# Zero rows up to 128 partitions for the scores and replications of a Mamba, attention and MoE kernel

## The reference

```python
# 1: Mamba over the 1024 pixels of an image, group norm, residual
xh = silu(causal_conv_k2(x @ W_in[:, :128]));  z = x @ W_in[:, 128:]
dt = softplus((xh @ W_x[:, :4]) @ W_dt + b_dt)          # 128 channels
h  = exp(dt * A) * h + dt * B * xh                       # 16 states per channel
y  = (sum_n h * C + xh * D) * silu(z);  x = x + silu(group_norm(y @ W_out))
# 2: causal attention over 1024 tokens, 8 heads of 8
t = t + softmax(mask(q @ k.T / sqrt(8))) @ v @ w_proj    # of layer_norm(t)
# 3: mixture of 8 experts, the best 2 of each token
t = t + sum_top2(p * (x @ expert_w + expert_b))          # of layer_norm(t)
```

## Time and profile before

| What | Value |
|---|---|
| median of three runs | 1631.68 us |
| the profiled execution: its own time | 1626.1 us |
| its span in the trace | 1624.0 us |
| TensorE matmul (PE) busy | 1260.7 us, 78% |
| VectorE (DVE) busy | 1171.9 us, 72% |
| ScalarE (ACT) busy | 704.3 us, 43% |
| GpSimd (POOL) busy | 512.2 us, 32% |
| mean granted TensorE clock | 0.761 of 2.4 GHz |
| DMA queues of the kernel | 14.6% of 16 engines' span |

### The profile page before, as it was taken

How to read it: one execution, slowest core, us unless ns; L and a number is a source line. 1 busy time by engine, 2 the same in 40 slices (tenths; PEclk the granted TensorE clock), 3 DMA queues, 4 the chain that set the end, 5 groups by cost and what they waited for, 6 DMA issues and landing times. The chain is left out here.

```text
span 1624.0 us, 17597 instructions
## 1 busy us (share of the span) xinstructions
PE 1260.7 (78%) x6388; PEld 499.9 (31%) x6388; DVE 1171.9 (72%) x1388; ACT 704.3 (43%) x1298; POOL 512.2 (32%) x272
## 2 busy tenths in 40 slices
PE   2455346888888987888887987888888988899894
PEld 1111111323233333333333323333233324433433
DVE  3396398787678968887679867887688867348345
ACT  1423322347434762376335642476326631460470
POOL 2454454344334332342243333342144321000000
PEclk9567556659966998589867997599758985695696
DMA  1100320021202111201211120201220120020000
GB/s 38 45 1 13 83 53 13 7 68 30 55 8 68 30 32 38 67 1 30 62 29 45 30 50 19 68 10 23 47 61 14 30 49 17 19 51 21 3 14 7
DMA packets 25863, 54.87 MB, mean 34 GB/s; under 512 B 8531, under 2 KB 8919, under 8 KB 23448
## 3 DMA queue, kind: packets, MB, share of 16 engines
q1 hardware_dynamic: 25776, 53.73, 14.6%
HBM read 28.15 MB, written 12.98 MB: 25 GB/s over the span
## 5 line engine op out<-in xcount | busy, mean ns | idle before, releaser
L926 DVE TENSOR_REDUCE row_max<-ps 128x1 f32<-128x768 f32 (+7 forms) x384 | 355.9, 952 | 142.2 <-PE ps L1202 139.6
L660 POOL TENSOR_TENSOR read<-state,c_rep 128x1024 f32<-128x1024 f32 x128 | 303.9, 2374 | 466.2 <-DVE state L970 450.6
L801 ACT ACTIVATE probs<-ps 128x512 f32<-128x512 f32 (+3 forms) x768 | 329.5, 496 | 144.7 <-PE ps L1305 86.5
L970 DVE TENSOR_TENSOR_SCAN state<-decay,drive 128x1024 f32<-128x1024 f32 x128 | 357.1, 2790 | 1.8 <-POOL read L660 1.1
L1198 PE MATMUL ps<-k_stack,q_stack 72*128 72x512 bf16 (+3 forms) x768 | 280.6, 456 | 83.2 <-DVE row_max L926 64.3
L1302 PE MATMUL ps<-q_stack,k_stack 75*128 75x512 bf16 (+3 forms) x768 | 222.8, 353 | 32.7 <-DVE drive L979 17.8
L979 DVE TENSOR_TENSOR drive<-ps,b_rep 128x512 f32<-128x512 f32 x256 | 169.6, 676 | 105.7 <-PE ps L1236 105.0
L762 ACT ACTIVATE decay<-ps,a_scale 128x512 f32<-128x512 f32 x256 | 175.3, 696 | 116.8 <-DVE state L970 100.1
L1236 PE MATMUL ps<-dt_rows,pick 96*128 96x512 bf16 x256 | 120.5, 471 | 96.9 <-DVE drive L979 69.5
L1317 PE MATMUL ps<-probs,v_aug 128*32 128x512 f32 (+3 forms) x1536 | 177.4, 536 | 4.1 <-ACT acc_sb L790 1.6
L1198 PEld LDWEIGHTS ps<-k_stack,q_stack 72*128 72x128 bf16 x768 | 73.8, 116 | 274.2 <-DVE row_max L926 171.4
(11 more groups left out here) (169 smaller groups left out, 1281.6 us busy)
## 6 DMA issues: line engine op xcount, KB each, us to landing
q_stack<-q_parts_dram SPq DMA_DIRECT2D x48, 192.0 KB
k_stack<-k_parts_dram SPq DMA_DIRECT2D x48, 192.0 KB
dt_rows<-read SPq DMA_DIRECT2D x96, 64.0 KB, 2.0
u_rows<-read SPq DMA_DIRECT2D x96, 64.0 KB, 2.0
k_parts_dram<-read SPq DMA_DIRECT2D x40, 128.0 KB, 2.4
q_parts_dram<-read SPq DMA_DIRECT2D x24, 128.0 KB, 2.3
xs<-in_x SPq DMA_DIRECT2D x8, 256.0 KB, 3.5
residual<-in_x SPq DMA_DIRECT2D x8, 256.0 KB, 9.6
```

What stands on the lines that cost most here:

```text
L660: pool.tensor_tensor(read[:, k % (2 * NG), :], state[:, k % 2, :], c_rep[:, :], ALU.mult)\
L801: act.activation(probs[:, e % (2 * QUAD), 0:w], bank_of(("scores", e))[:, 0:w], ACT.Exp, scale=SCALE).then_inc(exped.sem, 1)
L926: dve.tensor_reduce(row_max[:, i, h0:h0 + nh], scores[:, :, 0:P * (i + 1)], AX.X, ALU.max, negate=True).then_inc(row_maxed.sem, 1)
L970: dve.tensor_tensor_scan(state[:, k % 2, :], decay[:, k % 2, :], drive[:, k % 3, :], 0.0, ALU.mult, ALU.add).then_inc(scanned.sem, 1)
```

## The change

The score matmuls, the weighing matmuls and the replications take all 128 partitions of their operands. The partitions that held nothing are set so that they add nothing: `q_stack` from row 75, `dt_rows` and `u_rows` from row 96 and `pick` from row 96 are zero; `k_stack` has ones from row 72 on. Since the scores now read rows 72 to 74 too, where the maxima of the batch before stand, a copy of zeros from DRAM clears them with each load of the stacks, once per quad.

```diff
+    zeros_dram = nc.dram_tensor("zeros_dram", (3, 4, T), BF16, kind="Internal").ap()
-        pick = sb("pick", [96, JG, NS, CH], BF16)
+        pick = sb("pick", [P, JG, NS, CH], BF16)
-        dt_rows = sb("dt_rows", [96, NG, T], BF16)
-        u_rows = sb("u_rows", [96, NG, T], BF16)
+        dt_rows = sb("dt_rows", [P, NG, T], BF16)
+        u_rows = sb("u_rows", [P, NG, T], BF16)
 # SP, setup
                 assert setup_dmas[0] == LOADS
+                sp.wait_ge(zeros_set, 1)
+                sp.dma_start(zeros_dram[:, :, :], q_stack[64:67, 0:QUAD, :]).then_inc(zeros_out, 16)
 # DVE, setup
-                dve.memset(k_stack[64:96, :, :], 1.0).then_inc(dve_setup, 1)
+                dve.memset(k_stack[64:P, :, :], 1.0).then_inc(dve_setup, 1)
...
                 dve.memset(expert_start[:, :, 0:1], 0.0).then_inc(dve_setup, 1)
+                dve.memset(q_stack[64:P, :, :], 0.0).then_inc(zeros_set, 1)
+                dve.memset(dt_rows[96:P, :, :], 0.0).then_inc(zeros_set, 1)
+                dve.memset(u_rows[96:P, :, :], 0.0).then_inc(zeros_set, 1)
                 dve.wait_ge(weights_in, 16 * LOADS)
 # SP, the load of the stacks
                             heads = slice(quad * QUAD, (quad + 1) * QUAD)
+                            sp.wait_ge(zeros_out, 16)
+                            sp.dma_start(q_stack[KQ - 3:KQ, heads, :], zeros_dram[:, :, :])\
+                              .then_inc(stacks_in[quad].sem, 16)
 # PE, score_step
-                                last = pe.matmul(ps[:, bank, 0:w], q_stack[0:9 * DH, h0 + hh, tokens(i)],
-                                                 k_stack[0:9 * DH, h0 + hh, h * BANK:h * BANK + w],
+                                last = pe.matmul(ps[:, bank, 0:w], q_stack[:, h0 + hh, tokens(i)],
+                                                 k_stack[:, h0 + hh, h * BANK:h * BANK + w],
 # PE, the wait for the stacks
-                                pe.wait_ge(stacks_in[quad].sem, stacks_in[quad].at(b, 16 * 6))
+                                pe.wait_ge(stacks_in[quad].sem, stacks_in[quad].at(b, 16 * 7))
 # PE, weigh
-                            last = pe.matmul(bank[:, 0:w], k_stack[0:KQ, head, tokens(j)],
-                                             q_stack[0:KQ, head, lo:lo + w], start=True, stop=not diagonal)
+                            last = pe.matmul(bank[:, 0:w], k_stack[:, head, tokens(j)],
+                                             q_stack[:, head, lo:lo + w], start=True, stop=not diagonal)
```

More of the change, by code:

```diff
@@ L187, in mamba_attention_moe @@
         pool_chain = ctx.enter_context(nc.semaphore("pool_chain"))
+        zeros_set = ctx.enter_context(nc.semaphore("zeros_set"))
+        zeros_out = ctx.enter_context(nc.semaphore("zeros_out"))
         LOADS = 21
@@ L357, in mamba_attention_moe @@
         qk_parts_out = signal("qk_parts_out", 16 * 8)
-        stacks_in = [signal(f"stacks_in_{quad}", 16 * 6) for quad in range(2)]
+        stacks_in = [signal(f"stacks_in_{quad}", 16 * 7) for quad in range(2)]
         max_t_out = signal("max_t_out", 16)
```

## The result

| | before | after |
|---|---|---|
| median of three runs | 1631.68 us | 1569.51 us (1568.46 to 1570.04) |
| ratio, with its 95% interval | 1 | 0.9623 (0.9599 to 0.9646) |
| span of the profiled execution | 1624.0 us | 1566.7 us |
| mean granted TensorE clock | 0.761 | 0.851 |
| PE busy | 1260.7 us | 1124.4 us |

What follows compares the result with a forecast made beforehand. Score steps were taken as bound by DVE's reductions with PE at 2.4 GHz, by PE at 1.2 GHz. Gains of 53.5 us less 5.5 for setup make 48: 1631.7 - 48 = 1584 us, range 1560 to 1614.

Steps and rivals of the forecast that it cites:

- rival C: All stages: rows of zeros, or rows at all, don't count; only the setup's cost is left, 1637 us; chance 0.10.
- B: Score stages: the clock rises but falls back where PE waits for DVE's own work; 1609 us, chance 0.17.
- A: The forecast itself: padded rows lift PE's clock in scores and rounds; 1584 us, own range 1566 to 1602, chance 0.66.
- D: Whole kernel: all goes at 2.4 GHz, score stages left to DVE, rounds gaining too; 1555 us, chance 0.07.
- Term 1: Second quad of the score stages: waits at steps 36 to 38, last reductions and transposes shrink; 23 us, bounds 15 and 31.
- 2. steps 7 to 11, beside dt: First quad, steps 9 and 10 beside the dt product: 3.5 us in batches 0, 3 and 5, 10.5 us in all.
- Term 3: First quad, B and C products: 1.5 us of DVE's wait saved per batch, seven times, 10.5 us; bounds 0 and 17.5.
- 4. batch 7: Batch 7's score stage, with nothing beside the scores: 5.5 us gained, bounds 2 and 7.
- Term 5: Rounds, their clock already 0.88 and their start held by DVE's scans: 0.5 us each, eight times, 4 us; bounds 0 and 16.
- setup: Setup: three memsets ahead of DVE's first use of a weight delay the pipeline by 5.5 us; bounds 5.5 and 7.5.
- Rounds within 1 us of 103.6: Sign for the rounds: their time was expected to stay within 1 us of 103.6 us.
- What is late next: Shorter second quad against Mamba's chain to u's replication: 6 us free, 3.7 taken, so the chain does not take over.

## Why the prediction was right, and where it was not

The mechanism is the one forecast: the clock that PE is granted goes with the rows that its matmuls contract, and not with PE's busy share. The kernel with all costs and without the rows is 0.83% slower, the one with the rows 3.8% faster; rival C is out. B's 1609 us is out too. The 1569.5 us lie in A's own range of 1566 to 1602, but as near to D's 1555 us as to A's 1584. The clock does still fall in places, such as behind the wait for B's copy, and the stages hold 0.81 to 0.89 and not the 1.00 of D. That rows of zeros count, which was inferred from `pick` and the identities alone, is shown by the changed kernel and by the one with zeros on both sides.

The Trainium skill, "TensorE: Matmul & The Clock Gate", section "Part 1: The HAM clock gate", ties the clock to how busy PE has been and names no rows. The runs with 72, 96, 112 and 128 rows do not follow it: PE was busiest (44.01 of 50.90 us) where the clock was lowest (0.56), and least busy (30.62 of 45.20 us) where it was highest (0.89). A part of that busy time only follows from the clock, since PE takes longer over the same matmuls at 1.2 GHz; what decides is that the instructions of these kernels are the same but for the rows, and that the busier ones stayed slow. Here the measurement decides.

The terms, from the same steps of the two traces, over all batches:

| term | forecast | measured |
|---|---|---|
| 1. second quad (steps 32 to 40, and the end) | 23 us | 24.4 (23.0 + 1.4) |
| 2. steps 7 to 11, beside dt | 10.5 | 14.5, of it 11.2 in batches 0, 3 and 5 |
| 3. the B and C products (steps 15 to 21) | 10.5 | 3.0 |
| 4. batch 7 | 5.5 | 6.2 |
| 5. rounds, and the end of the span | 4 | 11.2 (7.2 + 4.0) |
| setup | -5.5 | -7.7 |

Batch 7's 6.2 us are contained in the rows of steps, which go over all batches. Without counting them twice the measured rows sum to 45.4 us. Steps 0 to 7 (4.2 us), 21 to 25 (4.3) and 25 to 32 (3.5), which have no term but that of batch 7 (3.9 of them are its), add 12.0, and that is the spans' difference of 57.3 us but for rounding. So it is in part luck that the forecast's 48 us came near the 57: its excess in term 3 stood against its lack in the rounds and in the steps it left out.

**Term 1** came out at its size, 22.3 us without batch 7, though not by its working. Batch 1 had 0.34 us ahead of both steps 37 and 38 and not of one, so the two waits of 1.60 us could give 2.5 us and not 2.9. The last reductions, which were given 0.5 us in each batch, gained 0.1.

**Term 3 was mis-sized, and its ground was wrong.** The prediction said that a part of the 3.49 us wait is ACT's copy of B "which remains", and took 1.5 us per batch from it. What remains is the time at which ACT gets to the copy, and not its duration: a faster PE is done sooner with B and waits longer, 3.98 us instead of 2.02, and behind the pause its clock is low for the C product. DVE's wait at step 20 grew to 5.50 us. The kernel with B's copy moved confirms it: the same steps then give 19.8 us.

**The stages of batches 2 to 5** were to come near 66 us and took 69.4 and 69.5. The 66 did not follow from the prediction's own terms, which take 3.7 and 1.5 us from batch 2's 73.7 and leave 68.5. The longest wait left in them is the one at step 20, 5.50 us in batch 2.

**Term 5 was mis-sized too.** "Rounds within 1 us of 103.6" failed: batch 2's rounds take 101.20 us. The prediction saw a clock of 0.88 and thought that little was left; the rounds with the 103.6 us became as short as the rest. With the scores' rows alone the rounds gain 3.5 us, with the rounds' rows alone 10.0, so the padding of `weigh` and `replicate` does something there. The whole change and the scores alone still take the same time: against the scores alone the whole change wins 3.7 us in the rounds and 3.2 behind the last score, and loses 4.3 in the setup, by its two more memsets, and 4.2 in the stages.

**The setup** costs 7.3 us where 5.5 were taken, near the upper bound of 7.5. DVE's timeline there:

```profile
15.61 3.47 DVE L243 MEMSET q_stack<- 64x4096 uint32 x1 [0.91 <-issue]
19.56 1.76 DVE L244 MEMSET dt_rows<- 32x2048 uint32 x1 [0.48 <-issue]
21.70 1.76 DVE L245 MEMSET u_rows<- 32x2048 uint32 x1 [0.38 <-issue]
23.50 0.60 DVE L250 SCALAR_TENSOR_TENSOR w_conv<-w_conv,conv_rows 64x128 f32<-64x128 f32 x2
```

The durations, 6.99 us, are as worked out (7.05); the pauses of 0.91, 0.48 and 0.38 us are what the value taken left out. 23.50 against 16.21 us is the 7.3.

**Right at nothing:** the padded matmuls take the same time. In the timeline of PE in the changed kernel, where the earlier trace rows has 75 and 96 rows:

```profile
532.85 0.38 PE L1313 MATMUL ps<-q_stack,k_stack 128*128 128x512 bf16 x1
...
534.64 0.38 PE L1247 MATMUL ps<-u_rows,pick 128*128 128x512 bf16 x1
```

The copies of zeros also cost nothing that a wait shows. The kernel with costs only has 3.7 us more in its stages, less than the 5.6 us by which a single stage of it differs from before, so no cost is shown by that either. "PE shows no wait for the stacks' DMAs at all" was not quite so, before or after: the weighing waits for the maxima on their way into `q_stack`, once for 0.8 us before and twice for 2.1 us in all in the changed kernel. These are not the copies of zeros, and the scores wait for no transfer into the stacks.

**What is late next** was answered wrongly. The prediction had 6 us free in the chain of u and 3.7 taken. It added one landing to the end of POOL's work at 668.1 us and left out SP, which first has to issue the four transfers of dt's last part. Those of u follow from 671.08 on, in the trace of the kernel before:

```profile
671.08 2.42 SPq L539 DMA_DIRECT2D u_rows<-read x4
```

The last of them landed at 674.89 us, so 1.2 us were free ahead of the replication at 676.14, and not 6. In batch 2 PE now waits 0.5 us for u's rows:

```profile
PE ps L1247 <- DMA u_rows<-read: 0.5, 1, 0.5
```

It does so in each of the six iterations that have a score stage and work of `c`, 0.5 to 1.3 us and 4.2 us in all, where before there was one such wait of 0.4 us. So the slack is used up. The kernels that moved B's copy show another price beside it: what they won at B came back at C's copy and at POOL's residual until these were moved too.

## What to carry to other kernels

Where TensorE's granted clock stays low though it is busy without a gap, look at how many rows its matmuls contract before looking at gaps: filling the partitions with zeros made no matmul longer here, and the operands only have to be cleared once, at a place where the engine waits anyway. And when one engine gets faster, look for the queue of the engine that frees its buffers: a copy that was in time before is then late, and moving it paid here only when the links behind it (C's copy, POOL's residual) were moved as well.

## What the hardware showed unexpectedly

The series of rows is not a straight line: batch 7, which has nothing but scores and masks, stays near 0.5 up to 96 rows (0.58), is at 0.65 with 112 and at 0.89 with 128, while the stages that have other products beside them take most of their gain from the first step, 24 rows in the scores with those in `replicate` and `weigh`. With the scores' rows alone the stages alternate between 66.1 us at about 0.94 (batches 2, 4) and 71.4 us at 0.81 (batches 1, 3, 5), and with the whole change batches 2 to 5 all take 69.4 or 69.5 at 0.88; why is open. The memsets of bf16 zeros stand in the trace with 32-bit elements, at 0.85 to 0.86 ns each whether they cover 64 partitions or 32 (3.47 us for 4096, 1.76 for 2048). The three are preceded by 0.38 to 0.91 us in which DVE waits for nothing that the profile shows, and the memset of `k_stack` by 1.76 us.
